# Two batches formed in one opening stage, and the adapter diagonal added by GpSimd

## The reference

```python
def reference(x, condB_coeff, itok_B_3_7, mask_Bx4096x4096_ik1, L0_cond_W, L0_cond_b, L1_cond_weight):
    def _L0_cond_ref(hidden_states, W, b, coeff, mask):
        output = jnp.einsum('bsi,oi->bso', hidden_states, W) + b
        sign = (2 * mask - 1).astype(hidden_states.dtype)
        diff = jnp.einsum('bsi,bio->bso', hidden_states, sign)
        return output + diff * coeff[:, None, None]
    def _L1_cond_ref(x, weight, adapter_ids):
        w = weight[adapter_ids]
        return jnp.einsum('bsi,boi->bso', x, w)
    x = x + _L0_cond_ref(x, L0_cond_W, L0_cond_b, condB_coeff, mask_Bx4096x4096_ik1)
    x = x + _L1_cond_ref(x, L1_cond_weight, itok_B_3_7)
    return x
```

## Time and profile before

| | |
|---|---|
| median of 3 runs | 422.56 us (422.48 to 426.25) |
| time of the profiled execution | 423.07 us |
| span of the profiled execution (first to last instruction) | 421.3 us, so 1.8 us lie outside it |
| mean granted TensorE clock | 0.992 |
| PE busy | 390.4 us (93%), 2496 matmuls and transposes |
| DVE busy | 366.6 us (87%), 400 instructions |
| ACT busy | 258.0 us (61%) |
| POOL busy | 6.0 us (1%) |
| DMA | 88.54 MB, mean 210 GB/s |

### The profile page before, as it was taken

One profiled execution on the slowest core, in us unless ns is written; L12 is line 12 of the kernel. 1 busy time (PEld: TensorE's weight loads), 2 busy tenths in 40 slices (PEclk: granted clock), 3 DMA queues, 4 the chain that ended last, 5 costly groups with the idle time before them and its releaser, 6 DMA issues.

```text
span 421.3 us, 6999 instructions
## 1 busy us (share of the span) xinstructions
PE 390.4 (93%) x2496; PEld 354.8 (84%) x2496; DVE 366.6 (87%) x400; ACT 258.0 (61%) x313; POOL 6.0 (1%) x14
## 2 busy tenths in 40 slices
PE   1979749999999999999999999999999999999777
PEld 1878748999899998999999998999999998999655
DVE  0455899999999999999999999999999999998740
ACT  3476765666676766667566766667566676665321
POOL 1111000000000000000000000000000000000000
PEclk9999979999999999999999999999999999999999
DMA  7998996988579874999779995999479975545211
GB/s 225 273 323 285 226 222 167 276 230 222 167 206 286 252 215 126 269 233 237 188 213 244 231 245 167 281 244 239 148 234 271 248 186 172 155 142 174 83 50 50
DMA packets 62451, 88.54 MB, mean 210 GB/s; under 512 B 7122, under 2 KB 48082, under 8 KB 62418
## 3 DMA queue, kind: packets, MB, share of 16 engines
q1 hardware_dynamic: 62418, 88.11, 78.9%
HBM read 79.70 MB, written 8.39 MB: 209 GB/s over the span
## 4 chain that ended last, share of the span: by engine, by line
PE 66%; DVE 18%; ACT 8%; DMA 3%; issue 2%; SPq 1%; ACTq 0%; DVEq 0%
PE first_ps L243 34%; PE second_ps L260 30%; DVE h_lo L396 6%; DVE natural L380 4%; DVE masks L360 4%; ACT masks L290 3%; DVE M_lo L365 2%; PE turn_ps L227 2%; DMA x_nat<-in_x_dram 2%; DVE w_lo L384 2%; ACT h_hi L316 1%; ACT w_hi L305 1%; DMA natural<-in_L_cond_weight_dram 1%; ACT M_hi L297 1%; ACT out_sb L323 1%
## 5 line engine op out<-in xcount | busy, mean ns | idle before, releaser
L243 PE MATMUL first_ps<-x_lo,M_hi 128*128 128x256 f32 x512 | 147.6, 288 | 10.0 <-DVE h_lo L396 6.0
L243 PE MATMUL first_ps<-x_hi,M_hi 128*128 128x256 f32 x512 | 145.6, 284 | 0.0
L243 PE MATMUL first_ps<-x_hi,M_lo 128*128 128x256 f32 x512 | 145.5, 284 | 0.0
L297 ACT CAST M_hi<-masks 128x1024 fp32r<-128x1024 f32 x64 | 67.2, 1050 | 117.6 <-DVE masks L360 117.6
L243 PEld LDWEIGHTS first_ps<-x_lo,M_hi 128*128 128x128 f32 x512 | 98.9, 193 | 13.2 <-issue 6.2
L260 PE MATMUL second_ps<-w_hi,h_lo 128*128 128x512 f32 x256 | 100.2, 391 | 5.0 <-DVE w_lo L384 2.8
L260 PE MATMUL second_ps<-w_hi,h_hi 128*128 128x512 f32 x256 | 99.9, 390 | 0.0
L243 PEld LDWEIGHTS first_ps<-x_hi,M_hi 128*128 128x128 f32 x512 | 98.9, 193 | 1.1
L260 PE MATMUL second_ps<-w_lo,h_hi 128*128 128x512 f32 x256 | 99.6, 389 | 0.0
L243 PEld LDWEIGHTS first_ps<-x_hi,M_lo 128*128 128x128 f32 x512 | 98.8, 193 | 0.0
L360 DVE SCALAR_TENSOR_TENSOR masks<-masks,coeffs,WT 128x1024 f32<-128x1024 f32 x64 | 81.8, 1278 | 13.0 <-ACT masks L290 9.5
(11 more groups left out here) (16 smaller groups left out, 128.1 us busy)
## 6 DMA issues: line engine op xcount, KB each, us to landing
masks<-in_mask_Bx4096x_ik_dram SPq DMA_DIRECT2D x64, 512.0 KB, 6.6
natural<-in_L_cond_weight_dram SPq DMA_DIRECT2D x256, 128.0 KB, 3.8
x_nat<-in_x_dram SPq DMA_DIRECT2D x8, 1024.0 KB, 7.8
out_dram<-out_sb SPq DMA_DIRECT2D x32, 256.0 KB, 3.3
natural<-in_L_cond_W_dram SPq DMA_DIRECT2D x8, 512.0 KB, 7.8
bias_col<-in_L_cond_b_dram SPq DMA_DIRECT2D x4, 1.0 KB, 5.3
coeffs<-in_condB_coeff_dram SPq DMA_DIRECT2D x1, 4.0 KB, 4.7
ids_row<-in_itok_B_dram SPq DMA_DIRECT2D x1, 0.0 KB
```

Source lines behind the costliest of these rows:

```text
L243: done = nc.tensor.matmul(acc(u), left, right, start=(k == 0 and u % 2 == 0 and j == 0), stop=(k == K - 1 and u % 2 == 1 and j == 2))
L297: nc.scalar.copy(by_chunk(M_hi, n), by_quadrant(masks[:, n % RING, :].bitcast(F32))).then_inc(M_hi_done, 1)
```

## The change

**One opening for batches 0 and 1.** A table gives the order of the first 16 chunks, (batch, chunk): after (0,0) and (0,1) the two batches take turns, batch 1 behind batch 0, so that each chunk of W^T serves two chunks of M as soon as it is there. The other 48 chunks keep their numbers.

**Places.** Two batches are accumulated at once: batch 0 in `first_ps`, batch 1's columns u = 0 to 3 in `second_ps` (`first`, 12 matmuls) and u = 4 to 7 in `turn_ps`. Since `turn_ps` is also where W and x are turned (`turned_W` has moved there from `second_ps`), the second half of each of batch 1's chunks is kept in `w_hi_right` and `w_lo_right` until all of W is turned, and then multiplied by a new step `rest(k)` (12 matmuls). W now has a place of its own, `W_nat`, under `w_hi_left` and `w_lo_left`. Batch 1's x arrives in `natural` and its halves go to `h_hi[:, 1]` and `h_lo[:, 1]`; odd chunks of batch 0 use `h_hi[:, 0]` and `h_lo[:, 0]`. The masks of the opening have 6 slots (two in `natural`). Batch 0's output quarters are accumulated in `first_ps`.

**Order.** All four streams of the opening are written out call by call. W and x transposes take turns in `turn_ps` under the tables `X_BEFORE_W` and `W_BEFORE_X`. x comes in halves of 512 KB. The small loads (coefficients, ids, bias) are issued by ACT instead of SP. In the main loop the second half of `turn_x(b + 1)` stands at i = 7 instead of i = 0 of the next batch. At n = 63 DVE turns two units ahead of `rest_h`, and the last four units follow it as turn, turn, rest, turn, rest, turn, rest, rest instead of turn, rest in turn.

**Diagonal.** `add_diagonal` runs on GpSimd for all 64 units; `turn_w` waits for it as before.

```diff
+OPENING = [(0, 0)] + [(0, (n + 1) // 2) if n % 2 else (1, n // 2 - 1) for n in range(1, 15)] + [(1, 7)]
+OPEN = len(OPENING)
+OPEN_RING = 6
+X_BEFORE_W = (0, 1, 1, 2, 2, 3, 4, 4)
+W_BEFORE_X = (1, 3, 5, 6)
...
+        def M_place(b, k, M, h, store):
+            if b >= 2:
+                return [(0, M[:, k % 2, :, :])]
+            if b == 0:
+                spare = h[:, 0, :K // 2, :].rearrange("p c (v q) -> p (c v) q", q=P)
+                return [(0, spare if k % 2 else M[:, 0, :, :])]
+            return [(0, M[:, 1, k % 2 * K // 2:(k % 2 + 1) * K // 2, :]),
+                    (K // 2, store[:, k, :].rearrange("p (u q) -> p u q", q=P))]
...
+        def acc(b, u):
+            at = slice(u % 2 * S, (u % 2 + 1) * S)
+            if b != 1:
+                return first_ps[:, u // 2, at]
+            return second_ps[:, u // 2, at] if u < K // 2 else turn_ps[:, u // 2 - 2, at]
...
             def load_mask(n):
+                b, k = chunk_of(n)
+                tile, loaded, _ = mask_place(n)
+                if n >= OPEN:
+                    sp.wait_ge(M_done, n - RING + 1)
+                elif n >= OPEN_RING:
+                    sp.wait_ge(M_done, n - OPEN_RING + 1)
+                sp.dma_start(tile, mask[b, k * P:(k + 1) * P, :]).then_inc(loaded, DMA)
...
             pool.wait_ge(ident_steps, 2)
...
+            pool.wait_ge(W_diag_added, K)
+            for g in range(CHUNKS):
+                if g:
+                    pool.wait_ge(w_diag_added, g)
+                add_diagonal(g)
...
+            def rest(k):
+                pe.wait_ge(M_done, slot_of(1, k) + 1)
+                if k == 0:
+                    pe.wait_ge(WT_done, K)
+                products(1, k, M_hi_place(1, k)[1], M_lo_place(1, k)[1]).then_inc(rest_done, 1)
...
             turn_W(0)
             turn_x(0, 0)
             turn_W(1)
-            turn_x(0, 1)
-            for n in range(CHUNKS + K):
+            turn_W(2)
+            first(0)
+            turn_x(1, 0)
+            first(1)
+            turn_W(3)
+            first(2)
+            turn_W(4)
+            first(3)
+            turn_x(0, 1)
+            first(4)
+            turn_W(5)
+            first(5)
+            turn_x(1, 1)
+            first(6)
+            first(7)
+            turn_W(6)
+            first(8)
+            first(9)
+            turn_W(7)
+            first(10)
+            first(11)
+            rest(0)
...
+            rest(5)
+            first(12)
+            first(13)
+            rest(6)
+            rest(7)
+            first(14)
+            first(15)
+            second(0, 0)
+            second(0, 1)
+            turn_x(2, 0)
+            second(0, 2)
+            turn_x(2, 1)
+            second(0, 3)
+
+            for n in range(OPEN, CHUNKS):
                 b, i = n // K, n % K
...
+                first(n)
                 if i == 4 and b + 1 < B:
                     turn_x(b + 1, 0)
-                if i % 2 and b:
+                if i == 7 and b + 1 < B:
+                    turn_x(b + 1, 1)
+                if i % 2:
                     second(b - 1, i // 2)
+            for t in range(4):
+                second(B - 1, t)
```

More of the change, by code:

```diff
@@ L89, in build @@
         first_done = sem("first_done")
+        rest_done = sem("rest_done")
         h_hi_done = sem("h_hi_done")
@@ L164, in _ @@
-            with nc.allow_non_contiguous_dma(reason="4 KiB of bias, once"):
-                for a in range(GRP):
-                    sp.dma_start(bias_col[a * SQ:(a + 1) * SQ, :],
-                                 bias[a * Q:(a + 1) * Q].rearrange("(u j) -> j u", j=SQ)).then_inc(bias_loaded, DMA)
-            sp.wait_ge(ids_loaded, DMA)
-            for n in range(CHUNKS + K + 2):
+            load_W(1)
+            load_mask(1)
+            load_mask(2)
+            load_mask(3)
+            load_W(2)
@@ L325, in _ @@
+            with nc.allow_non_contiguous_dma(reason="4 KiB of bias, once"):
+                for a in range(GRP):
+                    nc.scalar.dma_start(bias_col[a * SQ:(a + 1) * SQ, :],
+                                        bias[a * Q:(a + 1) * Q].rearrange("(u j) -> j u", j=SQ)
+                                        ).then_inc(bias_loaded, DMA)
+            sign(0)
             copy_WT(0)
-            sign(0)
             round_x(0, 0)
             round_M(0)
+            sign(1)
+            sign(2)
@@ L329, in _ @@
+            sign(3)
             copy_WT(1)
-            sign(1)
-            round_x(0, 1)
-            for n in range(CHUNKS + K + 2):
+            copy_WT(2)
+            round_M(1)
+            round_M(2)
+            round_x(1, 0)
+            round_M(3)
+            sign(4)
+            sign(5)
+            copy_WT(3)
+            sign(6)
+            sign(7)
+            copy_WT(4)
+            round_M(4)
+            round_M(5)
+            round_x(0, 1)
+            round_M(6)
+            round_M(7)
@@ new lines, in _ @@
+            sign(8)
+            copy_WT(5)
+            sign(9)
+            round_M(8)
+            round_x(1, 1)
+            round_M(9)
+            sign(10)
+            sign(11)
+            copy_WT(6)
+            round_M(10)
+            round_M(11)
+            sign(12)
+            sign(13)
+            copy_WT(7)
+            round_M(12)
+            sign(14)
+            sign(15)
+            round_w(0)
+            round_M(13)
+            round_w(1)
+            round_M(14)
+            round_w(2)
@@ new lines, in _ @@
+            round_M(15)
+            round_w(3)
+            round_h(0)
+            round_w(4)
+            sign(OPEN)
+            round_w(5)
+            round_h(1)
+            take_out(0, 0)
+            round_w(6)
+            round_w(7)
+            take_out(0, 1)
+            round_w(8)
+            round_x(2, 0)
+            round_M(OPEN)
+            sign(OPEN + 1)
+            take_out(0, 2)
+            round_w(9)
+            round_w(10)
+            round_x(2, 1)
+            take_out(0, 3)
@@ L403, in _ @@
             rest_M(0)
-            rest_x(0, 1)
-            dve.wait_ge(ident_steps, 2)
-            for n in range(CHUNKS + W_LAG):
-                b, i, g = n // K, n % K, n - W_LAG
+            add_sum(1)
+            add_sum(2)
+            add_sum(3)
+            rest_M(1)
+            rest_M(2)
+            rest_x(1, 0)
+            rest_M(3)
+            add_sum(4)
+            add_sum(5)
+            add_sum(6)
+            add_sum(7)
+            rest_M(4)
+            rest_M(5)
+            rest_x(0, 1)
@@ new lines, in _ @@
+            rest_M(6)
+            rest_M(7)
+            add_sum(8)
+            add_sum(9)
+            rest_x(1, 1)
+            rest_M(8)
+            rest_M(9)
+            add_sum(10)
+            add_sum(11)
+            rest_M(10)
+            rest_M(11)
+            add_sum(12)
+            turn_w(0)
+            add_sum(13)
+            add_sum(14)
+            add_sum(15)
+            rest_M(12)
+            turn_w(1)
+            rest_w(0)
+            turn_w(2)
+            rest_M(13)
@@ new lines, in _ @@
+            rest_w(1)
+            rest_w(2)
+            turn_w(3)
+            rest_M(14)
+            rest_M(15)
+            turn_w(4)
+            rest_w(3)
+            rest_h(0)
+            turn_w(5)
+            rest_w(4)
+            rest_w(5)
+            rest_h(1)
+            turn_w(6)
+            turn_w(7)
+            rest_w(6)
+            rest_w(7)
+            turn_w(8)
+            add_sum(OPEN)
+            turn_w(9)
+            rest_x(2, 0)
+            rest_w(8)
+            rest_M(OPEN)
```

369 lines of the change are left out of this document (244 added, 125 removed).

## The result

| | median, us (range, runs) | ratio to the kernel before, 95% interval |
|---|---|---|
| before | 422.52 (421.71 to 426.25, 4) | |
| changed | 412.97 (408.32 to 414.44, 4) | 0.9735 [0.9693, 0.9776] |

The change makes the kernel 9.55 us faster. All ratios in this text leave out two executions of later runs, 422.9 and 416.79 us, that took over 1.5% longer than the fastest of their kernel; medians and ranges hold them. The forecast was 404.0 with a range of 399.5 to 411.0: right in sign, 9.0 us too good, and the time lies outside the range. The profiled execution took 412.47 us with a span of 410.4 us.

A forecast was written before the change was run, and what follows sets the result against it. PE's own work was taken to bound the middle, 46.6 of 47.03 us a batch. 401.1 plus 0.6 restarts and 1.0 small loads made a 402.7 span; 1.8 outside, less 0.5 for medians, gave 404.0, range 399.5 to 411.

The forecast's parts named there:

- The opening: First 16 chunks, laid out engine by engine: last product ends at 73.9 us, a gain of 12.9 us.
- small loads: Coefficients, ids and bias on ACT's queue share the DMA engines from the start: 1.0 us taken, bounds 0 and 3.8.
- The first row: Start of the kernel: x's half and W's chunk 0 landed at 6 us, first transpose of W at 6.5.
- `first(0)` was said to run 19 to 22.5: Opening: batch 0's first product on PE starts at 19 us, after `turn_W(2)`, and ends at 22.5.
- the opening is late: Rival: the serial chain up to 39 us loses 4 to 6 us at engine handoffs, time 409; chance 0.12.
- What hides the loads: Opening's masks and first adapter units land before they are wanted; slot 10 lands about 37, wanted at 43.
- The middle of the kernel is bound by PE: Before the change, PE's own work fills 46.6 of a batch's 47.03 us; DVE close behind at 46.5.
- Six batches at 46.6: Main loop after the change: six batches take PE's own 46.6 us each instead of 47.03.
- x in halves, `turn_x` at i = 7: same work, 0: Batch boundary: moving the second half of x's transposes costs nothing; `rest_M` at T + 8.9 against PE's T + 9.2.
- POOL's hold: Main loop: each diagonal add on POOL costs DVE 0.18 us a unit, leaving DVE at 45.4 us a batch.
- both POOL rivals: Main loop: adds hold DVE 0.45 us each, 409.4, chance 0.13; or stop DVE longer, up to 443.8, slower, chance 0.03.
- The end: Last batch: both PE waits after `second(6,3)` and `second(7,1)` go, 5.1 us.

## Why the prediction was wrong, step by step

- **The opening** ("the opening's last product ends at 73.9"): measured 76.6, so 2.7 late, with 1.0 allowed for small loads. Two steps failed. The first row, "x's half and W's chunk 0 have landed at 6 us", transpose at 6.5: it was 7.88, 1.4 late. And `first(0)` was said to run 19 to 22.5 and ran 20.40 to 24.91, 1.0 longer. Reordering the first loads and ACT's first two calls gives back 1.0 to 1.2. The rival "the opening is late" was right in kind, though with 1.8 us and not 5: PE's work in hand after 39 us swallowed nothing of the delay.
- **What hides the loads.** This is the step that failed most. I followed each load up to the first `second` and none beyond, and did not ask what SP's order does to the DMA engines as a whole. Price: 3.8 us in the profiled execution, 3 to 5 by the two runs that remove it. No rival named it.
- **"The middle of the kernel is bound by PE".** For the kernel before it was wrong: DVE had 0.97 us of gaps in 47.03, all of them waits for ACT, and taking 0.3 us for each unit off it gave 46.61 (the run with the diagonal on POOL alone). I had priced DVE at 46.5 us a batch from the earlier trace rows, without those gaps, and read the chain's naming of PE as the bound. But from 341.69 to 348.51 the chain stands on DVE, through `rest_h`, the sum, `turn_w` and `rest_M`, and `first(b,1)` starts when that `rest_M` has ended. PE's wait did not appear in the list: it is the one stop of 0.3 us a batch shown above.
- **"Six batches at 46.6"**: they took 47.03, for another reason than before. "x in halves, `turn_x` at i = 7: same work, 0" was the failed step. I had placed `rest_h`'s end at T + 4.1 and, with the moved `rest_x` behind it, `rest_M`'s at T + 8.9, a cover of 0.3 us. With T = 239.62, `rest_h` ended at T + 4.8, since `sign` and `take_out` (0.47 us) stand ahead of `round_h`, and `rest_M` at T + 9.5: 0.3 late instead of 0.3 early. Cost 2.0 us.
- **POOL's hold**, 0.18 a unit: mechanism right, size too large. From 200 to 300 us 4 DVE instructions of 0.2 us more stand beside 17 adds, 0.05 a unit. DVE had room, so it cost nothing, and both POOL rivals fell.
- **The end**: right. Both waits went (5.1 in the sum; the new end alone gave 5.8 of span, 421.3 to 415.5, and 6.6 in the medians).
- **The wait of `second(0,0)` for `rest_h(0)`**, 0.4: 0.34. Right.
- **The sum as a whole.** With the start, the loads and the boundary mended the kernel takes 405.2, 1.2 above the forecast: the terms were sized well, in sum, for a kernel in which nothing new is late.

## What to carry to other kernels

After an edit of one stage, follow each queue one or two stages further than the edit: a load that stands behind a store's wait shows itself 50 us later, and a stretch in which the DMA share falls to half just ahead of one in which it is full is the sign of it. Where two engines stand within 1% of each other, do not take the one that the chain names as the bound: add up the gaps of the other over one period; if they are only short waits in a handshake, every place in its order counts. And look for a wait in the start times at the seam of two rows of matmuls, not only in the list of waits: a stop of 0.3 us behind a matmul of 0.28 was not in it.
